# Graph work of an attention loop in one burst per four steps, instead of one per two

## The reference

```python
xn = _layernorm(x, axis=-1)
x = x + gnn(xn, W1, b1, W2, b2, eps, src, dst) + mix(xn[None], W_qkv, W_out, b_out)[0]
x = x + ffn(_layernorm(x, axis=-1)[None], router_w, router_b, w1, b1, w2, b2)[0]
```

## Time and profile before

| | |
|---|---|
| median of 3 runs | 738.97 us (737.07 to 746.02) |
| profiled execution, its own time | 737.21 us |
| its span in the trace | 735.5 us |
| TensorE busy, of the span | 685.5 us, 93% |
| VectorE busy | 473.5 us, 64% |
| ScalarE busy | 233.7 us, 32% |
| attention steps 0 to 107 (with graph counts) | 147.18 to 386.37 us |

### The profile page before, as it was taken

One profiled execution on the slowest core, in us unless ns is written; L12 is line 12 of the kernel. 1 busy time (PEld: TensorE's weight loads), 2 busy tenths in 40 slices (PEclk: granted clock), 3 DMA queues, 4 the chain that ended last, 5 costly groups with the idle time before them and its releaser, 6 DMA issues.

```text
span 735.5 us, 12476 instructions
## 1 busy us (share of the span) xinstructions
PE 685.5 (93%) x3860; PEld 453.7 (62%) x3861; DVE 473.5 (64%) x1065; ACT 233.7 (32%) x472; POOL 153.4 (21%) x262
## 2 busy tenths in 40 slices
PE   4889999999999999999999999999998299999997
PEld 2545555455555555555555689898996177777742
DVE  4628752389897898887963897345444634445436
ACT  2222311123233232332332526060542143454310
POOL 6045210102132321302200600003112212322210
PEclk9998999999999999999999999999999599999978
DMA  9700000072634627090825930002019568844468
GB/s 295 210 0 0 1 3 1 0 288 75 231 142 162 229 77 262 29 350 13 304 99 207 354 157 1 1 1 86 30 58 366 227 215 303 286 140 131 130 206 294
DMA packets 48198, 109.70 MB, mean 149 GB/s; under 512 B 6694, under 2 KB 6710, under 8 KB 45680
## 3 DMA queue, kind: packets, MB, share of 16 engines
q1 hardware_dynamic: 38480, 85.41, 32.5%
q0 software_dynamic: 4256, 13.41, 5.0%
q10 hardware_dynamic: 5376, 9.93, 4.4%
HBM read 47.39 MB, written 61.35 MB: 148 GB/s over the span
## 4 chain that ended last, share of the span: by engine, by line
PE 80%; DVE 8%; DMA 4%; issue 3%; ACT 1%; POOL 1%; ACTq 1%; SPq 0%; DVEq 0%; POOLq 0%
PE bank L1361 12%; PE bank L1344 10%; PE bank L1312 9%; PE bank L1399 8%; PE bank L1278 7%; PE bank L1456 6%; PE bank L1522 6%; PE bank L1508 5%; PE bank L1323 5%; PE bank L1242 4%; PE bank L1384 4%; DMA arena<-slots 2%; DVE arena L918 2%; DMA arena<-in_wqkv 2%; PE bank L1532 2%
## 5 line engine op out<-in xcount | busy, mean ns | idle before, releaser
L918 DVE TENSOR_TENSOR arena<-iota,arena 125x384 f16<-125x384 f16 (+2 forms) x318 | 169.7, 593 | 23.3 <-PE bank L1242 14.0
L718 ACT ACTIVATE arena<-bank 128x416 f32<-128x416 f32 (+1 forms) x120 | 62.3, 519 | 146.9 <-PE bank L1344 143.9
L1361 PE MATMUL bank<-arena 128*64 128x416 f32 (+1 forms) x480 | 97.2, 524 | 3.2 <-DVE arena L971 2.8
L971 DVE TENSOR_SCALAR arena<-bank 128x416 f32<-128x416 f32 (+1 forms) x120 | 67.4, 586 | 42.8 <-PE bank L1344 42.7
L554 POOL COPY arena<-arena 125x12 f32 (+1 forms) x80 | 33.3, 417 | 230.8 <-DVE arena L918 136.1
L1312 PE MATMUL bank<-arena 128*128 128x416 f32 (+1 forms) x192 | 76.7, 548 | 2.9 <-DMA arena<-in_wqkv 1.5
L1242 PE MATMUL bank<-arena 125*128 125x160 f16 x471 | 51.7, 235 | 5.5 <-DVE arena L918 4.9
L1508 PEld LDWEIGHTS bank<-arena 128*128 128x128 f32 x448 | 52.8, 194 | 6.2 <-issue 6.2
L1312 PEld LDWEIGHTS bank<-arena 128*128 128x128 f32 x192 | 37.3, 203 | 31.0 <-issue 27.3
L1242 PEld LDWEIGHTS bank<-arena 125*128 125x128 f16 x471 | 32.5, 98 | 36.5 <-issue 27.2
L1361 PEld LDWEIGHTS bank<-arena 128*64 128x64 f32 x480 | 30.6, 135 | 36.4 <-issue 26.7
(11 more groups left out here) (247 smaller groups left out, 1184.8 us busy)
## 6 DMA issues: line engine op xcount, KB each, us to landing
slots<-arena SPq DMA_DIRECT2D x6, 5397.0 KB, 17.9
arena<-in_ew SPq DMA_DIRECT2D x16, 1024.0 KB, 6.3
slots<-arena SPq DMA_DIRECT2D x2, 5140.0 KB, 17.0
arena<-slots ACTq DMA_DIRECT2D x28, 257.0 KB, 3.0
arena<-in_x SPq DMA_DIRECT2D x8, 512.0 KB, 7.4
arena<-in_gw SPq DMA_DIRECT2D x2, 2048.0 KB, 16.7
arena<-in_wqkv SPq DMA_DIRECT2D x3, 1024.0 KB, 15.5
xn_rows<-arena SPq DMA_DIRECT2D x1, 2560.0 KB, 8.7
```

Source lines behind the costliest of these rows:

```text
L718: act.activation(probs[0:kt, s % NPB, 0, 0:n], bank[2 * (s % 2)][0:kt, 0:n], ACT.Relu).then_inc(p0_ready, 1)
L918: ins = dve.tensor_tensor(hot[:, :, c], iota16[0:CE, 0:width].unsqueeze(1).to_broadcast([CE, n, width]), window_cols[:, i % WBUF, of, k0:k ...
L971: dve.tensor_single_scalar(probs[0:kt, s % NPB, 1, 0:n], bank[2 * (s % 2) + 1][0:kt, 0:n], 0.0, op=ALU.max).then_inc(p1_ready, 1)
L1361: ins = pe.matmul(bank[AV][DH * a:DH * a + DH, 0:n], v_sb[0:kt, t, h * DH:h * DH + DH], probs[0:kt, s % NPB, a, 0:n], start=(t == 0), stop ...
```

## The change

After the three lists are filled, a function moves items of attention turns to the last of their four steps. For TensorE these are counts, sums and turns; for ScalarE the copies of windows and the saving of turned rows; for VectorE the forming of rows. VectorE's one-hots stay where they were. Items of the projection turns stay too. `summed` moves in the same way.

```diff
@@ -370,6 +370,19 @@
+        def gather(lists, kinds):
+            late = [[] for _ in lists]
+            for i, todo in enumerate(lists):
+                for item in todo:
+                    together = i >= NPRE and item[0] in kinds
+                    late[min((i - NPRE) // 4 * 4 + 3 + NPRE, len(lists) - 1) if together else i].append(item)
+            return late
+
+        pe_after = gather(pe_after, ("pair", "sum", "turn"))
+        act_after = gather(act_after, ("windows", "turn"))
+        dve_after = gather(dve_after, ("sum",))
+        summed = [(i - NPRE) // 4 * 4 + 3 + NPRE if i >= NPRE else i for i in summed]
+
         first_wo = (summed[-1] - NPRE + 2) | 1
```

## The result

The changed kernel takes 782.12 us (median of 3 runs, 781.57 to 784.51) against 738.97: a ratio of 1.0568 [1.0454, 1.0681], slower, and 1.5 us above the forecast. The profiled execution, the one that the forecast's sum was made for, took 781.57 us (1.0 above it), with a span of 779.8.

The account below looks back on a forecast made before the run. TensorE, busy for 93% of the span, was taken to bound the kernel, with VectorE close behind in the attention. The profiled 737.2 us plus 39.0 of cycle losses and 4.4 of clock gave 780.6 us, range 758 to 797.

Parts of the forecast that it names:

- The blocked half and the late relu: Attention bursts: VectorE's one-hot half waits for the burst's counts, delaying relus queued behind it; 4.6 us over steps 8 to 15.
- The walk: Hand-timed schedule of 30 four-step attention cycles at prices from the earlier trace; losses sum to 39.0 us.
- late entry: Five attention cycles that VectorE enters late, delaying the light pair's relu; 1.6 to 3.3 us each, 13.0 in all.
- turn behind its rows: Steps 36 to 39 and 76 to 79: the turn waits for rows moved to the loaded pair; 7.8 us in all.
- like steps 8 to 11: Three attention cycles where a blocked half delays the loaded pair's counts and relu; 3.6 us in all.
- few sums: Five attention cycles with few sums in the burst; 0.6 to 1.7 us each, 6.6 in all.
- ScalarE's copies: Three attention cycles whose sums also wait for ScalarE's copy of the windows; 2.8 us in all.
- sum bursts: Eight attention cycles with two to four groups of sums, which cover most of the late half; 3.9 us in all.
- clock, apart: At the two turns, 4.4 us of TensorE idling each lowers the clock; 2.2 us per fall, 4.4 in all.
- the rival of 796: Light attention pairs entered late add five more clock falls and chained lateness, 15 us above the forecast; chance 0.13.
- Exposure only: Rival: attention's ring hardly blocks, only the light pairs' 4.6 us wait for relus remains; 741.8 us, chance 0.12.
- Not slower: Rival: merged attention bursts save 2.7 us and cover VectorE's existing lateness of 6.5; 732.6 us, chance 0.05.

Follow-up runs that it names:

- e5_rows: Changed kernel, but rows of groups 3 and 6 formed where they were before the change; 774.0 us, 1.0494 of the kernel before.
- e7_warm: Changed kernel with 24 unused matmuls put ahead of the turns of groups 3 and 6; 782.7 us, 1.0618 of the kernel before.
- e10_warm12: Changed kernel with 12 unused matmuls put ahead of the turns of groups 3 and 6; 782.68 us in a single execution.
- e11_no_check: e9_sums_rows without TensorE's branches for edges beyond the usual number and the sums behind them; 733.17 us, 0.9968 of the kernel before.
- e9_sums_rows: Changed kernel with only sums, turns and saves gathered, counts not, and rows of groups 3 and 6 in their old place; 739.09 us, 1.0016.
- e6_ring3_rows: Changed kernel with a ring of three windows from window 18 and rows of groups 3 and 6 in their old place; 745.23 us, 1.0114.

## Why the prediction was right, step by step

**The blocked half and the late relu.** The walk gave steps 8 to 11 9.58 and 12 to 15 10.92. In its times: the half 21.1 at 5.80 (170.18 - 164.28, the start of step 8's scores, is 5.90), values at 8.03 (8.17), VectorE 3.27 late into the next cycle (3.30), light values at 4.00 (178.03 - 174.00 = 4.03). That VectorE's queue is kept in order, as the Trainium skill says in "TensorE: Matmul & The Clock Gate", section "Architectural detail: the array is 16× 32×32, not 1× 128×128", agrees with this: no relu passed a blocked half. The class sums, with what each cost after the change:

| class (cycles) | walked | measured |
|---|---|---|
| late entry (12, 24, 52, 64, 92) | 13.0 | 16.8 |
| turn behind its rows (36, 76) | 7.8 | 12.4 |
| like steps 8 to 11 (8, 48, 88) | 3.6 | 3.8 |
| few sums (28, 40, 68, 80, 104) | 6.6 | 6.8 |
| ScalarE's copies (16, 56, 96) | 2.8 | 2.8 |
| sum bursts (eight) | 3.9 | 4.6 |
| last three | 1.3 | 1.3 |
| clock, apart | 4.4 | in the first two |
| sum | 43.4 | 48.4 |

**The clock was the mis-sized term.** It was about the right size for one fall (2.2 taken; 1.9 measured at a turn, 1.5 in cycle 12), but I counted two. There were four: cycles 12, 36, 52 and 76 exceed the walk by 1.8, 2.2, 1.7 and 2.4 (52 walked like 12, 76 like 36), together 8.1 for the 4.4. At the measured prices the four falls are 6.8 of this, an estimate; the rest is not the clock's. The table by stretch after the change, at steps 12 to 14, at the turn of group 3, and in cycles 52 and 76 (the number behind the busy times is the granted clock):

```profile
174.00:178.00 4.00, 1.40 (x14) 1.05 (x13) 3.96 (x8) 1.03 (x2) 0.75 (x2) 1.00 0.00 0
178.00:182.00 4.00, 3.98 (x20) 2.39 (x20) 1.41 (x3) 0.52 (x1) 0.43 (x2) 0.66 0.00 0
...
247.00:250.40 3.40, 0.05 (x1) 0.05 (x1) 3.37 (x7) 0.00 (x0) 1.60 (x2) 0.58 0.00 0
250.40:252.00 1.60, 1.60 (x10) 1.29 (x12) 0.93 (x2) 0.00 (x0) 0.00 (x0) 0.50 0.00 0
...
288.50:291.80 3.30, 2.83 (x8) 0.85 (x8) 1.85 (x4) 0.00 (x0) 1.47 (x5) 0.50 0.00 0
356.80:363.50 6.70, 4.39 (x16) 2.04 (x16) 3.26 (x6) 0.00 (x0) 1.08 (x4) 0.50 0.61 208
```

After 2.6 us of idling in four, the clock is 0.66 in the next four, mostly at the lower level of 1.2 GHz, and the scores at 179.83 show it (0.71 for 0.46). In `e5_rows`, where the clock holds in this cycle (1.00, with its light values waiting 2.60), it takes 11.21 instead of 12.70. None of `e5_rows`, `e7_warm` and `e10_warm12` changes steps 12 to 15, and the clock fell there after the change and in `e7_warm` (12.70 both), not in `e5_rows` and `e10_warm12` (11.21 both). So with the same order and the same wait a fall comes in one execution and not in the next; why is open. The step that failed is the line between forecast and rival: falls in light pairs entered late were put into the rival of 796 alone. Two of its five came in the profiled execution, and of its 4 us of further lateness little: 1.3 us of the excess lie outside these four cycles.

**The branches** were missing from the walk, and mattered little: the class of sum bursts came out 0.7 above its 3.9. `e11_no_check` shows their price in `e9_sums_rows`. In the changed kernel's own trace three sums behind a branch start late, by 0.4 us together, nearly all of it in cycle 32.

**Outside the stage** I took nothing. The executions differ there by 4.1 us in favour of the changed one (1.4 ahead, 2.7 behind), and this hides most of the 5.0 that the attention came out above the sum. That the forecast is nearer than its terms is luck. The lower end of the range, 758, is 739 plus half of 39; from the sum's own 737.2, and with the clock's 4.4 kept, it would have been 761.

**The rivals.** Exposure only would have been nearer with a longer ring and early rows: `e6_ring3_rows` loses 7.9 us in the attention where that rival had 4.6. Not slower: bursts of sums alone cost nothing in the attention once their branches are out (`e11_no_check`, 3.0 us under the kernel before), bursts of counts do. The advice to batch matmuls back to back, from the Trainium skill's "Perfetto Trace Analysis", section "Matmul Optimizations", found nothing to gain: the clock was 1.00 before, and 0.96 with the bursts.

**The signs in the profile.** Waits for relus and one-hots are 32.9 us on TensorE (30 and more foreseen), with the rows ahead of the turns 42.3; VectorE's idling on counts went from 0.6 to 63.1; twelve light pairs last 3.16 to 3.18, the others are those entered late or with a block to split; the turns wait 4.2 and 5.2 (4 foreseen). All as told, but for the steps after the attention: foreseen unchanged, they took 2.7 us less in this execution.

## What to carry to other kernels

Before work is gathered into bursts, ask who refills what the burst consumes: a ring of two windows that fits a burst of 1.2 windows blocks its producer at 2.4, and everything behind the blocked instruction in that in-order queue comes late, the work of other loops too. Lengthen the ring together with the burst, or leave the consumer spread. If something is gathered, let it be work that no refill waits for (the sums here), and look at the branches in the burst first. Here even that was not shown to gain; spreading the sums gained half a per cent.

## What the runs showed of the hardware

- A branch in TensorE's queue costs in some places and not in others. Sums that follow each other by 0.23 us stood 0.98 apart behind one in `e9_sums_rows`; of its 36 branches in the attention 29 cost nothing, and in the kernel before none costs anything. In the trace's records of the sequencer, half of the loads of the value take 0.3 us and half 0.9 to 1.0; load, compare and branch take 0.84 to 1.71 us in all, at the upper end more than the 1.04 of the four sums that stand between two branches.
- The clock fell after 12 fillers as it did without them, later (from 248.1 on); with 24 it fell while they ran, and was back for the turn. In cycle 12 the same instructions with the same wait of 2.6 us kept the clock in two of four executions.
- Behind the attention the same instructions took 322.6 to 329.0 us from one profiled execution to the next. A difference of a few us is better read from the stage's own cycles than from a few total times.
